# A four-layer graph network on one core: an edge sort without its product, counts two units ahead, GpSimd's share of the one-hots of places, and one-hots four ahead in the first layer

## The reference

```python
edge_index = jnp.stack([src, dst])
x = _layernorm(x + _L0_gnn_ref(x, edge_index, edge_type_64, ...))
x = _layernorm(x + _L1_gnn_ref(x, src, dst, edge_weight, ...))
x = _layernorm(x + _L2_gnn_ref(x, edge_index, edge_type_2, ...))
x = _layernorm(x + _L3_gnn_ref(x, edge_index, ...))
# L0: the mean of relation messages over the incoming edges
msg = (x[src] + rel_emb[edge_type]) @ W_msg.T + b_msg
agg = segment_sum(msg, dst) / max(deg, 1)
out = x @ W_self.T + b_self + agg
# L1: weighted attention over edges; L2: one of two maps by edge type, relu; L3: sum normalized by degrees
```

## Time and profile before

| | us |
|---|---|
| median of 3 runs (lowest, highest) | 4307.43 (4306.51, 4310.26) |
| the profiled execution's own time | 4305.91 |
| its span, first to last instruction | 4304.2 |
| sort, 60 to 1127: busy PE / DVE / ACT / POOL | 697.50 / 1021.99 / 387.25 / 179.29 |
| first layer's pass, 1150 to 1885: busy PE / DVE / ACT / POOL | 697.39 / 559.92 / 394.70 / 107.67 |

### The profile page before, as it was taken

One profiled execution on the slowest core, in us unless ns is written; L12 is line 12 of the kernel. 1 busy time (PEld: TensorE's weight loads), 2 busy tenths in 40 slices (PEclk: granted clock), 3 DMA queues, 4 the chain that ended last, 5 costly groups with the idle time before them and its releaser, 6 DMA issues. The chain is left out here.

```text
span 4304.2 us, 94469 instructions
## 1 busy us (share of the span) xinstructions
PE 3657.9 (85%) x38991; PEld 3057.2 (71%) x38992; DVE 3648.7 (85%) x4714; ACT 2047.2 (48%) x4002; POOL 431.4 (10%) x335
## 2 busy tenths in 40 slices
PE   2665666666599999968999999997999999989998
PEld 2554555555466666648999999996888888867776
DVE  7999999999877777768999999998666666778897
ACT  2333333333355555532333333333666666757776
POOL 3002221230111111110000000001000000000000
PEclk9778899998799999978999999998999999989999
DMA  3000000000032222210000000001333333300000
GB/s 103 1 1 1 2 2 1 2 2 2 31 117 108 108 108 108 108 58 2 2 2 2 2 2 2 2 2 39 101 103 102 101 100 101 97 1 10 5 10 10
DMA packets 104807, 178.63 MB, mean 42 GB/s; under 512 B 11690, under 2 KB 101559, under 8 KB 104244
## 3 DMA queue, kind: packets, MB, share of 16 engines
q1 hardware_dynamic: 103892, 170.07, 12.1%
q10 hardware_dynamic: 480, 2.40, 0.2%
HBM read 86.93 MB, written 85.49 MB: 40 GB/s over the span
## 5 line engine op out<-in xcount | busy, mean ns | idle before, releaser
L97 DVE TENSOR_TENSOR both_hot<-iota_own,recs 128x1792 bf16<-128x1792 bf16 (+1 forms) x686 | 756.5, 1106 | 252.4 <-PE rR L1437 143.1
L1801 ACT ACTIVATE gC<-qC 128x896 f32<-128x896 f32 x343 | 314.6, 917 | 647.3 <-PE qC L1821 647.3
L1833 PE MATMUL qO<-A,gC 128*128 128x132 f32 x4802 | 615.2, 280 | 0.0
L593 PE MATMUL pV<-VO,PM 128*128 128x70 bf16 (+4 forms) x6524 | 295.3, 210 | 326.1 <-issue 322.7
L1833 PEld LDWEIGHTS qO<-A,gC 128*128 128x128 f32 x4802 | 566.4, 190 | 0.0
L593 PEld LDWEIGHTS pV<-VO,PM 128*128 128x128 bf16 x6524 | 272.3, 107 | 350.2 <-issue 348.8
L1445 PE MATMUL rO<-sl_f,terms 128*128 128x512 bf16 (+1 forms) x2058 | 500.1, 354 | 4.1 <-ACT sl_f L1403 2.5
L91 DVE TENSOR_TENSOR PM<-iota_b,place 128x3584 bf16<-128x3584 bf16 (+1 forms) x226 | 480.5, 2126 | 0.8 <-ACT place L455 0.8
L2145 ACT ACTIVATE some_r<-rC 128x512 fp32r<-128x512 f32 (+1 forms) x686 | 336.1, 543 | 253.0 <-PE rC L2175 252.6
L1403 ACT ACTIVATE sl_f<-rC 128x896 bf16<-128x896 f32 x343 | 314.0, 916 | 279.9 <-PE rC L1425 279.7
L91 DVE TENSOR_TENSOR places_hot<-iota_own,recs 128x896 bf16<-128x896 bf16 x700 | 403.2, 620 | 51.8 <-PE tC L2414 21.4
(11 more groups left out here) (296 smaller groups left out, 6083.9 us busy)
## 6 DMA issues: line engine op xcount, KB each, us to landing
tables<-sl_f SPq DMA_DIRECT2D x343, 224.0 KB, 1.9
sl_f<-tables SPq DMA_DIRECT2D x343, 224.0 KB, 2.5
edges<-terms SPq DMA_DIRECT2D x1, 3528.0 KB, 11.2
B<-in_x SPq DMA_DIRECT2D x1, 2744.0 KB
out<-B SPq DMA_DIRECT2D x7, 392.0 KB
terms<-in_edge_type ACTq DMA_DIRECT2D x2, 686.0 KB
terms<-in_edge_weight ACTq DMA_DIRECT2D x1, 686.0 KB
recs<-in_src SPq DMA_DIRECT2D x1, 686.0 KB
```

The source lines that it names most:

```text
L97: return v.tensor_tensor(o.rearrange("p n k (a b) -> p (n k) a b", b=2), iota_own[:, 0:w].rearrange("p (a b) -> p a b", b=2).unsqueeze(1). ...
L593: mm = pe.matmul(pV[n % 2][:, g * row:(g + 1) * row].rearrange("p (f b) -> p f b", f=u.nf), PM[:, n % 2, col, :], values[:, :, col, :], st ...
L1833: mm = pe.matmul(pO[i % SUMS][:, 0:XW], Cs[:, U % 2, j, :], A[:, a, :], start=a == 0, stop=a == NT - 1)
```

## The change

- The product goes. TensorE's count gets one more matmul, with `lift` (2048 on the diagonal): the count of a record's own digit is raised by 2048. ScalarE's copy out of PSUM becomes Relu with bias -2048 (`drop`), which leaves the wanted count and zeros elsewhere, straight into M. R goes, M has two buffers, O three.
- Counts, one-hots O and the copies out of PSUM run two units ahead instead of one, and `double` three instead of two. ScalarE's order is now place(n), evict(n-1), double(n+3), looked(n+2); VectorE's rank(n), hot(n+2), VO(n), PM(n); TensorE's count(n+2), route(n).
- SHARE = 2: GpSimd makes the last two columns of each unit's PM, one TENSOR_SCALAR of 128 numbers each, from `iota_b` and the rank. It waits for s_pair(n) and s_out(n-2), and signals s_rest_perm, for which route(n), rank(n+2) and place(n+2) wait. VectorE makes 30 or 26 columns. GpSimd's other work is spread over the units behind these.
- First layer: AHEAD = 4, and five buffers (HOTS) instead of three.

```diff
-            O = sb("O", [P, 2, 512], BF16, c1)
-            R = sb("R", [P, 2, 512], BF16, c1)
-            M = sb("M", [P, 512], BF16, c1)
+            O = sb("O", [P, 3, 512], BF16, c1)
+            M = sb("M", [P, 2, 512], BF16, c1)
...
+                    for n, u in enumerate(units):
+                        cols = u.npos * u.ngrp
+                        gp.wait_ge(s_pair, n + 1)
+                        if n >= 2:
+                            gp.wait_ge(s_out, n - 1)
+                        for c in range(cols - SHARE, cols):
+                            ins = gp.tensor_scalar(PM[:, n % 2, c, :], iota_b[:, 0:P], rank[:, n % 2, c:c + 1], None, ALU.is_equal)
+                        ins.then_inc(s_rest_perm, 1)
+                        m, when = divmod(n - SPLIT_AT - 1, 2)
+                        if 1 <= m <= NB and when == 0:
+                            low_last(m - 1)
+                        if 0 <= m < NB and when == 0:
+                            low_first(m)
+                        for d in range(LATE):
+                            if n == done_with[d] + 3:
+                                weight_rest(gp, d)
+                                kinds(gp, d)
...
-                            act.wait_ge(s_mul, n - 1)
-                        act.activation(R[:, n % 2, 0:k], pR[n % 2][:, 0:k], ACT.Copy).then_inc(s_look, 1)
+                            act.wait_ge(s_taken, n - 1)
+                        act.activation(M[:, n % 2, 0:k], pR[n % 2][:, 0:k], ACT.Relu, bias=drop[:, 0:1]).then_inc(s_look, 1)
...
+                        pe.matmul(pR[n % 2][:, 0:k], lift[:, :], O[:, n % 3, 0:k], start=False, stop=False, skip_group_check=True)
...
                         pe.wait_ge(s_perm, n + 1)
+                        pe.wait_ge(s_rest_perm, n + 1)
...
-                            if n + 1 < b:
-                                count(n + 1)
+                            if n + 2 < b:
+                                count(n + 2)
...
-                            v.tensor_tensor(M[:, 0:cols * u.w], O[:, n % 2, 0:cols * u.w], R[:, n % 2, 0:cols * u.w], ALU.mult).then_inc(s_mul, 1)
-                            if n + 1 < b:
-                                hot(n + 1)
                             ranks(n)
+                            if n + 2 < b:
+                                hot(n + 2)
...
-                            equal(v, PM[:, n % 2, 0:cols, :], place[:, n % 2, 0:cols, :], cols, P).then_inc(s_perm, 1)
+                            equal(v, PM[:, n % 2, 0:cols - SHARE, :], place[:, n % 2, 0:cols - SHARE, :], cols - SHARE, P).then_inc(s_perm, 1)
...
-            AHEAD, FOUR = 2, 4
+            AHEAD, HOTS, FOUR = 4, 5, 4
...
-                            if U >= 3:
-                                v.wait_ge(s_o, U - 2)
+                            if U >= HOTS:
+                                v.wait_ge(s_o, U - HOTS + 1)
```

More of the change, by code:

```diff
@@ L232, in gnn_four_layers_kernel @@
             done_with = {u.d: n + 1 for n, u in enumerate(units) if u.level == 3}
+            mores_of = {n: 3 * i for i, n in enumerate(n for n, u in enumerate(units) if u.extra is not None)}
             SPLIT_AT, LIN_AT = A_N + 2, A_N + 28
@@ L236, in gnn_four_layers_kernel @@
             PADDED = 96
+            SHARE = 2
+            LIFT = 2048.0
+            assert 8 * P < LIFT and DIG * P < LIFT
             LATE = ND1 - 2
@@ L526, in _ @@
                         double(a + 1)
+                        double(a + 2)
                         looked(a)
+                        looked(a + 1)
                         for n in range(a, b):
@@ L531, in _ @@
                                 evict(n - 1)
-                            if n + 1 < b:
-                                looked(n + 1)
                             i, sub = slot_of(n)
@@ L544, in _ @@
                                 act.activation(B[:, i, :], pL[:, 1, :], ACT.Copy).then_inc(s_own, 1)
+                            if n + 3 < b:
+                                double(n + 3)
                             if n + 2 < b:
-                                double(n + 2)
+                                looked(n + 2)
                             if n == A_N - 8:
@@ L1424, in table @@
                             for j in range(n):
-                                mm = pe.matmul(pC[U % 2][:, tile_in_group(m, j), :], both_hot[:, U % 3, j, 1, :], both_hot[:, U % 3, j, 0, :],
+                                mm = pe.matmul(pC[U % 2][:, tile_in_group(m, j), :], both_hot[:, U % HOTS, j, 1, :], both_hot[:, U % HOTS, j, 0, :],
                                                start=m > 0 or j != 1, stop=m > 0 or j != 0, skip_group_check=True)
@@ L1436, in relation @@
                                 to = tile_in_group(m, j) * RELW
-                                return pe.matmul(pR[:, to:to + DW], both_hot[:, U % 3, j, 0, :], rel_hot[:, K % 2, a % FOUR * n + j, 0:DW],
+                                return pe.matmul(pR[:, to:to + DW], both_hot[:, U % HOTS, j, 0, :], rel_hot[:, K % 2, a % FOUR * n + j, 0:DW],
                                                  start=a == 0 and j == 0, stop=a == NT - 1 and (m > 0 or j != 0), skip_group_check=True)
```

84 lines of the change are left out of this document (41 added, 43 removed).

## The result

The changed kernel takes **4311.9 us** in the median of 20 runs (4303.14 to 4332.05), the kernel before 4303.76 in 20 runs beside it (4299.44 to 4313.77). The ratio is 1.0019 (95% interval 1.001 to 1.0027). The forecast was 69 us faster; it is 8 us slower. The profiled execution has a span of 4315.0 us.

A forecast was written before the change was run, and what follows sets the result against it. VectorE was taken to bound the sort, TensorE the first layer's pass. Sort terms summed to -57 us and the pass to -12, together -69 from 4305.9: 4238 us as a median, range 4208 to 4268 (8 in 10: 4200 to 4325).

The forecast's parts named there:

- GpSimd's queue: Sort: GpSimd's shares wait behind its other work, some 0.7 us for each of 14 instructions: +10 us (0 to +30).
- the later end of PM: Sort: route starts some 0.5 us later, covered except where ScalarE writes finished groups: +10 us (0 to +40).
- the columns' effect on VectorE: Sort: GpSimd's two columns delay VectorE by 0.15 us a unit over 226 units: +34 us (0 to +72).
- rival 1: Sort: GpSimd is starved and each unit stalls by one column: 4328 us, chance 0.16; half-way 4286 us, 0.16.
- my three signs of being wrong: GpSimd columns over 1 us unobstructed, VectorE's long instructions delayed over 0.3 us a unit, or the pass's waits staying.
- product, one matmul more, Relu: Sort: VectorE's product goes, -63 us; one more matmul in each count and Relu for Copy, both at 0.
- counts two ahead, phase start: Sort: more lead removes 20 of 28.3 us of waits before products, -20 us; the second phase starts later, +3.
- the share, all in all: Sort: two columns fewer for VectorE -31 us, GpSimd's columns +34, its queue +10, later end of PM +10.
- first layer four ahead: First layer's pass: waits for one-hots -24 us, later close at six borders +12, together -12 us (-24 to +5).
- the new wait for close: First layer's pass: close stands behind three make, so TensorE's sums start 1.95 us later at six borders: +12 us.
- Rival 2: Sort: ScalarE's chain becomes the bound, PM waits 0.3 us for place in each unit: 4306 us, chance 0.10.
- Rival 3: Sort: GpSimd's work is free, both columns fall into openings and nothing queues: 4190 us, chance 0.08.

The follow-up runs named there:

- aside_memset: The changed kernel, but VectorE makes all columns of PM and GpSimd clears two unread tiles of that size, waits and signals kept: 4245.81 us.
- aside_spread: aside_memset with GpSimd's work on a finished group spread one instruction a unit over nine units: 4193.09 us.
- share_one: The changed kernel with GpSimd making one column of each unit's PM instead of two: 4237.32 us.
- share_one_spread: share_one with GpSimd's work on a finished group spread one instruction a unit over nine units: 4185.55 us.
- after: The changed kernel as it is, with the whole change against the kernel before: 4311.9 us.
- share_spread: The changed kernel, two columns by GpSimd, with only GpSimd's work on a finished group spread one instruction a unit over nine units: 4270.31 us.
- no_share: The changed kernel with SHARE = 0: VectorE makes all columns of PM and nothing waits for GpSimd's columns: 4180.99 us.
- one_ahead: no_share with counts, one-hots and copies out of PSUM one unit ahead instead of two: 4213.0 us.
- ahead_only: The kernel before with only the first layer's one-hots four ahead: 4287.33 us.
- no_share_close: no_share with a new group's first relations made two units later and the last of the one-hots behind close: 4165.14 us.

## Why the prediction failed, point by point

Two steps failed, both terms of the share. The first is **GpSimd's queue**, the term of +10 (0 to +30). The runs give it 53 to 55 us in the sort (`aside_memset` less `aside_spread`, `share_one` less `share_one_spread`, after less `share_spread`). I had priced fourteen long instructions at 0.7 us and let "a unit of slack" cover the groups' short ones. In fact the waits ahead of them count as well, the 4.20 us for recs in the rows above, and instructions that wait there hold the columns of the units behind. It is some 5 us for each of the 11 groups.

The second, and the dearer, is **the later end of PM**, the term of +10 (0 to +40). I had route start 0.5 us later and said that this is covered except where ScalarE writes finished groups. The mechanism was right, and it is where the time goes; the size was wrong. With two columns GpSimd has no gap left in a unit, so route starts 1.32 us late in the median and 2.5 or more in a quarter of the units, and the granted clock is lower where that falls together (0.79 in the eleven units, 0.95 with one column). That is 75 us in the sort with the queue spread. What I priced well was the columns' effect on VectorE: 0.15 a unit, and VO is 0.10 longer, and two columns lose 0.4 to 2.3 us in 48 units against `no_share`, which with the 0.135 saved makes 0.14 to 0.18. The 0.11 us that the prediction gave as an estimate for one column is far too low: the shortest of 452 took 0.60. What VectorE does to GpSimd stood only in rival 1, as a stall at the rank, and not in the sum. The rest between `no_share` and one column with spread work is 6 us in the sort, within what two executions of the same code differ by.

The range was drawn too narrow as well: 4208 to 4268 is less than the bounds of GpSimd's price alone (-34 to +38 about 4238), and those of the queue and of the later end (20 and 30 more) lie outside it. Nor did my three signs of being wrong help: columns of over 1 us with nothing in their way (0.60), VectorE delayed by more than 0.3 us a unit (0.10), waits of the pass that stay (they fell). None came, since they ask about single instructions and about the pass, and none about a queue.

| term, us | forecast | shown |
|---|---|---|
| product, one matmul more, Relu | -63 | -86 (`one_ahead`, with the other edits named there) |
| counts two ahead, phase start | -17 | -22 (`no_share` less `one_ahead`) |
| the share, all in all | -31 + 34 + 10 + 10 = +23 | +136 |
| of it GpSimd's queue | +10 | +55 |
| of it the second column, queue spread (the later end of PM) | +10 | +75 |
| sort | -57 | +28 |
| first layer four ahead | -12 | -22 |

- *The product.* Row to row the unit became 0.30 us shorter in level 1 (median from rank to rank 4.80 before, 4.50 in `no_share`) as forecast; at 392 numbers it is 4.10 to 3.77, 0.33 instead of 0.27. That makes 69 of the 86; the other 17 fall in units that are longer than the median and I can't assign them.
- *Counts ahead.* Of the waits before the products, 11.6 + 16.7, those at the rank are 6.1 in `no_share`: right.
- *The first layer.* TensorE's wait for both_hot fell as forecast from 41.3 to 17.3, and the new wait for close is there: 11.9 us in five places and 2.2 in the sixth in the changed kernel, whose trace lacks 124 of these matmuls; 13.0 in six, 2.2 at the longest, in `ahead_only`, where none is missing (forecast 12 in six, 1.95 each). The waits of the pass in the changed kernel, then its timeline at the end of a group:

```profile
PE rC L1449 <- DVE both_hot L97: 17.3, 7, 14.4
...
PE rR L1461 <- DVE A L1237: 11.9, 5, 2.4
```

```profile
1482.03 0.56 PE L1449 MATMUL rC<-both_hot 128*128 128x128 bf16 x7 [0.49 <-DVE both_hot L97]
...
1483.93 1.14 DVE L1237 TENSOR_TENSOR A<-A,rO 128x512 f32<-128x512 f32 x2
...
1484.97 0.19 PE L1461 MATMUL rR<-rel_hot,both_hot 128*128 128x65 bf16 x1 [2.38 <-DVE A L1237]
```

  Both terms held, and the pass still gained 22 instead of 12. The two stretches from the sort's end to gm, before and then `ahead_only`, with the same 7478 matmuls:

```profile
1142.60:1934.80 792.20, 719.02 (x7478) 492.28 (x7478) 584.70 (x722) 403.84 (x822) 118.59 (x94) 0.96 0.27 101
```

```profile
1148.50:1918.50 770.00, 707.47 (x7478) 487.94 (x7478) 582.36 (x722) 402.22 (x822) 107.24 (x94) 0.96 0.28 104
```

  TensorE stands idle for 73.2 us and then 62.5, 10.7 less, which is what the two terms gave. The other 11.6 us are busy time, which I had taken as fixed. The weight loads' own row of the waits fell by more than the matmuls' 24.0, by 32.8 (before, then after):

```profile
PEld rC L1425 <- DVE both_hot L97: 51.3, 62, 14.6
```

```profile
PEld rC L1449 <- DVE both_hot L97: 18.5, 8, 14.5
```

  That matmuls with late weights are counted as busy, and that this makes most of the 11.6, is my reading. `no_share_close` then won 16.1 in this stretch: of the 13.0 us for close none is left, and of the 17.3 for both_hot only the 14.4 at the start.
- *Rival 1*, that every unit stalls by one column, is not what happened: ordinary units are as short with two columns as with none (medians 4.46 and 3.73 us in `share_spread`, 4.50 and 3.77 in `no_share`; in the changed kernel 4.46 and 3.95). Its sign, VectorE idle at the rank because of GpSimd, came to 25.7 us and not to the 60 I had set. Its time, 4328, lies 16 us from the measured one, which is luck: the road was another.
- *Rival 2*, ScalarE's chain, showed its sign (58.8 us before PM, with place) and its time (4306), and its mechanism, a late route that holds the queue of ScalarE, is the one seen. The low clock that I named for it is in the trace too (0.58 in unit 144), but behind route's wait for GpSimd, and not by itself. Its 0.3 us in each unit are in truth several us at each finished group, so that its time, 6 us from the measured one, is luck in part. I gave it a chance of 0.10.
- *Rival 3*, that GpSimd is free, holds for one column in level 1 and nowhere for two.

## What to carry to other kernels

A share moved to an idle engine joins a queue: count for that engine what stands ahead of each piece, with the waits of those instructions, and not only what it does to its neighbour. An average of 17% busy said that GpSimd had room; it had none for something that a chain needed every 3.7 us, since it was either shut out or standing at a wait. Take the engine's time for one piece as it is beside the neighbour's work, multiply by the pieces in a period, and if that is the period, don't do it: ordinary units may show nothing, and the lateness comes out wherever a third engine has side work. And where an order puts side work in a bunch ahead of what a chain waits for, spreading it one piece a period is the first thing to try: it gave 42 to 53 us here without a change in the work.

## What was unexpected of the hardware

- GpSimd's comparison of 128 numbers, 0.60 us undisturbed, is held up for as long as VectorE runs two-input instructions back to back, 3.91 us in the median of level 1 with one column (`share_one_spread`), and comes through when the one-input rank reduction starts. I had expected it to get in at a border as in the earlier trace rows. The Trainium skill (GPSIMD Engine Reference, section 8, Key points) says that GpSimd contends with VectorE instructions that have two SBUF inputs; the trace agrees, and it shows more than contention, since in `share_one_spread` VectorE loses nothing (VO 1.54) and GpSimd everything.
- A GpSimd memset of the same tile isn't held up: 0.194 us at the shortest, 0.204 in the median, beside the same VectorE instructions (`aside_memset`).
- Relu with a bias, out of PSUM, takes 0.09 us more than the plain copy took for 392 numbers: 0.59 against 0.50, and so in the mean of 121 each (588 and 497 ns).

```profile
341.81 0.59 ACT L468 ACTIVATE M<-pR,drop 128x392 bf16<-128x392 f32 x1 [0.72 <-PE pR L606]
```
